# Attention scores from two float32r parts in half of the array's rows, in place of three bfloat16 parts in all of them

## Chip, cores and metric

The kernel runs on one core of a Trainium2 chip. The metric is the device time of one execution in microseconds (us); lower is better. The engines are named as in the profile: PE is TensorE's matmul side and PEld its weight loads, DVE is VectorE, ACT is ScalarE, POOL is GpSimd, SP the engine that issues the DMAs.

## The reference

```python
qn = layer_norm(Q, ln_q_g, ln_q_b)                  # Q: 16 x 512 x 256, all float32
q = (qn @ Wq + bq).reshape(B, 512, 16, 16)          # 16 heads of 16
k = (KV @ Wk + bk).reshape(B, 1601, 16, 16)         # KV: 16 x 1601 x 256
v = (KV @ Wv + bv).reshape(B, 1601, 16, 16)
scores = einsum('bhqd,bhkd->bhqk', q, k) / sqrt(16)
attn = softmax(scores, axis=-1)
ctx = einsum('bhqk,bhkd->bhqd', attn, v)
x = Q + (ctx @ Wo + bo)
h = layer_norm(x, ln_ff_g, ln_ff_b)
out = x + silu(h @ W1 + b1) @ W2 + b2               # W1: 256 x 1024
```

## The kernel before, in words

There are 16 batches. A batch is worked off in 4 quarters of 4 heads, a quarter in 13 key tiles of 128 keys (the last has 65), a tile in two units. So a batch has 52 tiles.

**Scores.** A number of q or k is split into three bfloat16 parts (`k_parts`, `q_parts`). For each head, `k_stack` and `q_stack` hold six blocks of 16 rows, so that one matmul over 96 rows sums the six products of parts that matter. Three more rows hold ones (in `k_stack`) and the negated row maximum in three parts (in `q_stack`), so that the matmul over 99 rows at L1010 gives scores less the maximum, keys on partitions and 512 queries on the free side. ACT takes the exponential of two heads at a time (L717) into `probs`. Then `multiply_v` (L1029) multiplies by v, in float32, for four heads: each head's v has 32 columns, and the four heads go to the four quarters of PSUM's partitions.

**Maxima.** The row maximum has to be known before the scores are made. So PE also makes every score the other way round, queries on partitions (L995: 128 queries by 512 keys, 96 rows), into one of two PSUM buffers (`rows_ps`); DVE reduces each to one column (L830). A quarter has 52 of these steps: 48 of 512 keys and 4 that hold the last 65 keys of four heads. They run up to two quarters ahead, 4 in each tile. At the end of a quarter DVE negates the maxima and splits them (L832 to L844), PE turns them (`turn`, L944), ACT copies them to `shift_parts` and SP places them in `q_stack` (`place_shift`).

**Side work.** All other products of PE go through one PSUM bank, `side`, one step after the other: transposes of context and x (`ctx`, `x`, `h`), the k, q and v projections, the output projection (`wo`), and the two layers of the MLP (`w1`, `w2`). Lists written out by hand (`PREPARE`, `FINISH`, `TURN`) give each step the units in which its products are made. `plan` sets PE's order in a tile: the two score matmuls of a unit first, then the unit's side products, the v product of the tile before at the end of the second unit, and the four maximum matmuls spread by cost among these.

**Stacks.** For k and q, ACT writes the whole number and the first part (L662, L663), POOL makes the second and the third part (L513 to L516), and SP moves the parts to the stacks: 24 small DMAs for the first copies in each quarter's group of heads (`place`), then 6 that copy a block within the stack (`repeat`).

## Time and profile before

| | |
|---|---|
| time, median of 3 runs | 3768.38 us (3765.79 to 3769.14) |
| time of the profiled execution | 3763.43 us |
| its span, first to last instruction | 3761.6 us |
| granted TensorE clock, mean | 0.989 |
| busy share: PE, PEld, DVE, ACT, POOL | 95%, 43%, 66%, 60%, 24% |
| chain that ended last: PE, DVE, ACT | 81%, 11%, 4% |

A quarter takes 53 to 60 us and a batch 224.9 us, the same to a few ns in every batch but the first and the last. PE's busy time counts each matmul until its modelled end, so that matmuls that follow one another closely overlap in it; the distance between two starts says more than the duration.

### The profile page before, as it was taken

Reading aid. Unit: us, or ns where it says so; the run is one execution under the profiler, and the core shown is the slowest. Engines: PE = TensorE matmul, PEld = TensorE weight load, DVE = VectorE, ACT = ScalarE, POOL = GpSimd, SP = SyncE. Lnnn points to the kernel's source line nnn. Section 1 sums busy time; section 2 is a strip of 40 time slices with the busy share of each in tenths; the row PEclk is TensorE's granted clock in tenths of the full one; section 3 lists DMA queues with packets and bytes.
Section 4 is the critical chain, followed back from the end, with each engine's and each line's share of the span. In section 5 each row is a group of like instructions: output and inputs, shape, how many; then the busy total and the mean of one; then the engine's idle time right before and its main releaser. Section 6 shows DMA issues by size and latency. Waiting matters only on the chain.

```text
span 3761.6 us, 52959 instructions
## 1 busy us (share of the span) xinstructions
PE 3559.0 (95%) x19880; PEld 1605.0 (43%) x19880; DVE 2483.2 (66%) x4568; ACT 2242.9 (60%) x2979; POOL 901.5 (24%) x1323
## 2 busy tenths in 40 slices
PE   3899999999999999999999999999999999999996
PEld 2233444444434444444444434444444444444434
DVE  2777767666676766667666676766667676676751
ACT  1366666656666565666656666566656656666562
POOL 2122313212231222313122231212313112231101
PEclk8899999999999999999999999999999999999999
DMA  3222212222122321212222122322212232121200
GB/s 84 45 50 40 46 32 61 41 47 45 32 51 39 65 41 32 47 33 58 41 58 38 30 50 37 64 41 36 49 32 54 42 64 39 27 48 34 41 7 12
DMA packets 121409, 162.99 MB, mean 43 GB/s; under 512 B 36912, under 2 KB 102464, under 8 KB 118080
## 3 DMA queue, kind: packets, MB, share of 16 engines
q1 hardware_dynamic: 121152, 159.60, 21.7%
q8 instruction: 157, 2.57, 0.3%
q14 instruction: 100, 0.82, 0.1%
HBM read 46.43 MB, written 8.39 MB: 15 GB/s over the span
## 4 chain that ended last, share of the span: by engine, by line
PE 81%; DVE 11%; ACT 4%; issue 2%; SPq 1%; POOL 1%; DMA 0%; ACTq 0%; POOLq 0%; DVEq 0%
PE o_ps L1029 20%; PE rows_ps L995 19%; PE scores L1010 14%; DVE chunk_max L830 8%; PE side L972 6%; PE side L969 6%; PE side L958 5%; PE side L950 4%; PE side L962 3%; ACT probs L717 2%; PE side L954 2%; DVE stats L748 1%; DVE resid L775 1%; PE side L941 1%; ACT ctxT L633 1%
## 5 line engine op out<-in xcount | busy, mean ns | idle before, releaser
L830 DVE TENSOR_REDUCE chunk_max<-rows_ps 128x1 f32<-128x512 f32 (+1 forms) x3328 | 2124.4, 666 | 1132.9 <-PE rows_ps L995 1124.4
L717 ACT ACTIVATE probs<-scores 128x1024 f32<-128x1024 f32 (+1 forms) x1664 | 1676.0, 1023 | 1174.5 <-PE scores L1010 1167.1
L995 PE MATMUL rows_ps<-k_stack,q_stack 96*128 96x512 bf16 (+1 forms) x4096 | 1220.1, 339 | 94.1 <-DVE chunk_max L830 50.6
L1010 PE MATMUL scores<-q_stack,k_stack 99*128 99x512 bf16 (+1 forms) x3328 | 1033.6, 379 | 3.3 <-ACT probs L717 2.7
L1029 PE MATMUL o_ps<-probs,v_sb 128*32 128x512 f32 x6656 | 886.5, 605 | 0.4 <-ACT probs L717 0.4
L995 PEld LDWEIGHTS rows_ps<-k_stack,q_stack 96*128 96x128 bf16 x4096 | 334.3, 97 | 1164.2 <-DVE chunk_max L830 930.7
L1010 PEld LDWEIGHTS scores<-q_stack,k_stack 99*128 99x128 bf16 (+1 forms) x3328 | 325.0, 100 | 300.4 <-issue 38.2
L513 POOL TENSOR_TENSOR rest<-whole,k_parts 128x512 f32<-128x512 f32 (+1 forms) x128 | 120.6, 942 | 1002.4 <-ACT k_parts L663 997.2
L565 POOL TENSOR_TENSOR attT<-o_sb,denom 128x512 f32<-128x512 f32 x64 | 81.2, 1268 | 945.3 <-DVE denom L817 945.3
L969 PE MATMUL side<-hT,w_sb 128*128 128x256 f32 x1024 | 272.6, 380 | 11.8 <-ACT tanh_sb L675 9.9
L972 PE MATMUL side<-w_sb,ffT 128*128 128x256 f32 x1024 | 259.2, 381 | 5.6 <-DVE ffT L793 5.0
L1029 PEld LDWEIGHTS o_ps<-probs,v_sb 128*32 128x32 f32 x6656 | 131.0, 108 | 296.8 <-issue 222.2
L958 PE MATMUL side<-wv_sb,ctxT 128*128 128x128 f32 (+1 forms) x1664 | 242.3, 278 | 4.6 <-ACT v_sb L649 2.0
L958 PEld LDWEIGHTS side<-wv_sb,ctxT 128*128 128x128 f32 (+1 forms) x1664 | 226.0, 187 | 46.7 <-ACT v_sb L649 11.4
L950 PE MATMUL side<-ctxT,wk_sb 128*128 128x512 f32 (+1 forms) x512 | 222.7, 519 | 9.2 <-ACT k_parts L663 9.2
L969 PEld LDWEIGHTS side<-hT,w_sb 128*128 128x128 f32 x1024 | 192.9, 190 | 63.2 <-ACT tanh_sb L675 17.0
L972 PEld LDWEIGHTS side<-w_sb,ffT 128*128 128x128 f32 x1024 | 191.5, 189 | 56.5 <-issue 7.7
L673 ACT ACTIVATE ffT<-side,half_b 128x256 f32<-128x256 f32 x256 | 121.5, 475 | 111.5 <-PE side L969 108.8
L528 POOL TENSOR_TENSOR newton<-rstd 128x2 f32<-128x2 f32 (+1 forms) x144 | 28.1, 195 | 591.6 <-DVE half_var L763 584.0
L962 PE MATMUL side<-wo_pad,attT 128*128 128x256 f32 x512 | 139.7, 389 | 5.0 <-POOL attT L565 3.9
L675 ACT ACTIVATE tanh_sb<-side,half_b 128x256 f32<-128x256 f32 x256 | 121.7, 475 | 0.0
L514 POOL TENSOR_TENSOR k_parts<-whole,k_parts 128x512 bf16<-128x512 f32 (+1 forms) x128 | 121.1, 946 | 0.1
(68 smaller groups left out, 1971.3 us busy)
## 6 DMA issues: line engine op xcount, KB each, us to landing
k_stack<-k_parts SPq DMA_DIRECT2D x768, 50.0 KB, 2.2
k_stack<-k_stack SPq DMA_DIRECT2D x192, 200.1 KB, 5.6
ctx_nat<-in_ctx SPq DMA_DIRECT2D x48, 512.0 KB, 4.0
q_stack<-q_parts SPq DMA_DIRECT2D x768, 16.0 KB, 1.8
q_stack<-q_stack SPq DMA_DIRECT2D x192, 64.0 KB, 3.4
x_nat<-in_x SPq DMA_DIRECT2D x16, 512.0 KB, 6.1
resid<-in_x SPq DMA_DIRECT2D x32, 256.0 KB, 2.8
out<-resid SPq DMA_DIRECT2D x32, 256.0 KB, 2.5
```

The costliest lines, as they stand in the source:

```text
L673: nc.scalar.activation(ffT[:, m, :], side[:, cols], ACT.Identity, bias=half_b1[:, m:m + 1], scale=0.5)
L675: last = nc.scalar.activation(tanh_sb[:, cols], side[:, cols], ACT.Tanh, bias=half_b1[:, m:m + 1], scale=0.5)
L717: nc.scalar.activation(probs[0:rows, (q + t) % 2, 2 * LQ * pair:2 * LQ * (pair + 1)], scores[0:rows, 2 * LQ * pair:2 * LQ * (pair + 1)], A ...
L830: nc.vector.tensor_reduce(dst, src, AX.X, ALU.max).then_inc(rows_read, 1)
L950: ins = nc.tensor.matmul(side[:, 0:width(arg)], wk_sb[:, j, P * s:P * (s + 1)], ctxT[:, j, CHUNK * arg:CHUNK * arg + width(arg)], start=(j ...
L958: ins = nc.tensor.matmul(side[0:rows, P * t:P * (t + 1)], ctxT[:, j, P * i:P * i + rows], wv_sb[:, j, P * s:P * (s + 1)], start=(j == 0), ...
L962: ins = nc.tensor.matmul(side[:, D * i:D * (i + 1)], attT[:, j, q0:q0 + P], wo_pad[:, j, :], start=(j == 0), stop=(j == 3))
L969: ins = nc.tensor.matmul(side[:, QH * i:QH * (i + 1)], w1_sb[:, j, P * m:P * (m + 1)], hT[:, j, :], start=(j == 0), stop=(j == KC - 1))
L972: ins = nc.tensor.matmul(side[:, D * i:D * (i + 1)], ffT[:, j, P * i:P * (i + 1)], w2_sb[:, j, :], start=(j == 0), stop=(j == FM - 1))
L995: last = nc.tensor.matmul(rows_ps[:, m % 2, d0:d0 + w], q_stack[s][0:STACK, h, P * t:P * (t + 1)], k_stack[s][0:STACK, h, k0:k0 + w], star ...
L1010: ins = nc.tensor.matmul(scores[0:keys_in(t), LQ * j:LQ * (j + 1)], k_stack[s][:, h, P * t:P * t + keys_in(t)], q_stack[s][:, h, :], start ...
L1029: last = nc.tensor.matmul(o_ps[32 * j:32 * j + 32, :], v_sb[q // 2][0:rows, t, col:col + 32], probs[0:rows, (q + t) % 2, LQ * j:LQ * (j + 1)],
```

## The change

- Each number is split into **two float32r parts** (float32r is a 4-byte type that the matmul reads as it is). Three blocks of 16 rows hold the three products that matter, so a head takes 48 rows for the maxima and 50 for the scores (two rows of shift).
- A head lies in **one half of the array's rows**: even heads in rows 0 to 49, odd heads in rows 64 to 113. A stack is [128, 4 pairs, keys].
- `plan` puts each score matmul **next to a maximum matmul of the other half**, and spreads these pairs: score, maximum, part of the first unit's side products, score, maximum, the rest of them; then score, maximum, v product, score, maximum, the second unit's side products.
- The maximum steps alternate between the halves; the last chunk of keys takes 66 keys in place of 65.
- `read_parts` on POOL is one subtraction in place of three. `repeat` is gone: `place` writes each of the three blocks from `k_parts` and `q_parts` (24 DMAs in a group, of 4-byte numbers). `place_shift` issues four DMAs in place of three.
- Negating the maxima takes three DVE instructions in place of seven; `turn` is one float32 transpose in place of four bfloat16 matmuls, and ACT copies 32 x 128 in place of 12 x 512.
- DVE sets the whole of `k_stack` to one at the start, and SP waits for that before it fills the stacks.

```diff
-PARTS = 3
-K_ROWS = (0, 0, 0, 1, 1, 2)
-Q_ROWS = (0, 1, 2, 0, 1, 0)
+PARTS = 2
+K_ROWS = (0, 0, 1)
+Q_ROWS = (0, 1, 0)
+HALF = 64
+PAIRS = HH // 2
-PLACED = 2 * 4 * PARTS
-REPEATED = 2 * (len(K_ROWS) - PARTS)
+PLACED = 2 * 4 * len(K_ROWS)
...
-TAIL = width(NCH - 1)
-M_STEPS = [step for r in range(M_ROWS) for step in [(r, c) for c in range(NCH - 1)] + [(r, None)] * (r % 4 == 3)]
+TAIL = width(NCH - 1) + 1
+M_STEPS = [step for p in range(2) for step in
+           [(e, p, t, c) for t in range(QT) for c in range(NCH - 1) for e in range(2)] + [(e, p, None, None) for e in range(2)]]
...
+PARTNER = (1, 0, 1, 0)
 def plan(steps):
-    units, slot = [], 0
+    units = []
     for t in range(KT):
-        work = []
-        for u in (2 * t, 2 * t + 1):
-            work += [(u, "scores", j) for j in range(2)]
-            work += [(u, "side", product) for product in products_at(steps, u)]
-            work += [(u, "pv", None)] * (u % 2)
...
+        fill = [[("side", product) for product in products_at(steps, u)] for u in (2 * t, 2 * t + 1)]
+        tile = []
+        for n in range(2):
+            first, second = 2 * n, 2 * n + 1
+            cost = [COST[what[1]] for _, what in fill[n]]
+            cut = 0
+            while cut < len(cost) and sum(cost[:cut]) * 2 < sum(cost):
+                cut += 1
+            middle = [("pv", None)] if n == 1 else fill[n][:cut]
+            unit = [("scores", PARTNER[first]), ("max", PER_TILE * t + first)] + middle
+            unit += [("scores", PARTNER[second]), ("max", PER_TILE * t + second)] + fill[n][0 if n == 1 else cut:]
+            tile.append(unit)
+        units += tile
     return units
...
-        k_stack = [sb(f"k_stack{s}", [ROWS, HH, LK], BF16) for s in range(2)]
+        k_stack = [sb(f"k_stack{s}", [P, PAIRS, LK], F32R) for s in range(2)]
...
             def place(dst, src, rows, g):
-                for part in range(PARTS):
-                    slot = rows.index(part)
+                for slot, part in enumerate(rows):
                     for h in range(4 * (g % 2), 4 * (g % 2) + 4):
-                        sp.dma_start(dst[16 * slot:16 * slot + 16, h, :], src[16 * h:16 * h + 16, part, :])\
-                            .then_inc(placed[g], 16)
+                        first = HALF * (h % 2) + 16 * slot
+                        sp.dma_start(dst[first:first + 16, h // 2, :].bitcast(F32),
+                                     src[16 * h:16 * h + 16, part, :].bitcast(F32)).then_inc(placed[g], 16)
...
-                repeat(b, 2 * s)
                 place(q_stack[s], q_parts, Q_ROWS, 2 * s + 1)
-                repeat(b, 2 * s + 1)
...
+                sp.wait_ge(ones_set, 4)
                 fill_stacks(0, 0)
...
-                wait(pool, split, b * 10 + n)
-                seq.inc(nc.gpsimd.tensor_tensor(rest[:, 0:w], src, first, ALU.subtract))
-                seq.inc(nc.gpsimd.tensor_tensor(second, src, first, ALU.subtract))
-                pool.wait_ge(pool_seq, seq.value)
-                nc.gpsimd.tensor_tensor(parts[:, 2, off:off + w], rest[:, 0:w], second, ALU.subtract).then_inc(split, 1)
+                nc.gpsimd.tensor_tensor(parts[:, 1, off:off + w], whole[:, n % 2, 0:w],
+                                        parts[:, 0, off:off + w].bitcast(F32), ALU.subtract).then_inc(split, 1)
...
             def make_rows(b, q, m):
-                r, c = M_STEPS[m]
-                s = q // 2
+                e, p, t, c = M_STEPS[m]
+                s, pair, rows = q // 2, 2 * (q % 2) + p, slice(HALF * e, HALF * e + STACK)
...
-                    last = nc.tensor.matmul(rows_ps[:, m % 2, d0:d0 + w], q_stack[s][0:STACK, h, P * t:P * (t + 1)],
-                                            k_stack[s][0:STACK, h, k0:k0 + w], start=True, stop=True)
+                    last = nc.tensor.matmul(rows_ps[:, m % 2, d0:d0 + w], q_stack[s][rows, pair, P * tile:P * (tile + 1)],
+                                            k_stack[s][rows, pair, k0:k0 + w], start=True, stop=True)
...
             def make_scores(b, q, u, n, first):
...
-                j = 2 * (u % 2) + n
-                h = 4 * (q % 2) + j
+                j, pair, rows = 2 * (u % 2) + n, 2 * (q % 2) + u % 2, slice(HALF * n, HALF * n + ROWS)
                 ins = nc.tensor.matmul(scores[0:keys_in(t), LQ * j:LQ * (j + 1)],
-                                       k_stack[s][:, h, P * t:P * t + keys_in(t)], q_stack[s][:, h, :],
+                                       k_stack[s][rows, pair, P * t:P * t + keys_in(t)], q_stack[s][rows, pair, :],
                                        start=True, stop=True)
```

## Rows read from the trace of the kernel before

**Rows 1.** The page: busy time by engine, clock in 40 slices, start of the chain.
```profile
PE 3559.0 (95%) x19880; PEld 1605.0 (43%) x19880; DVE 2483.2 (66%) x4568; ACT 2242.9 (60%) x2979; POOL 901.5 (24%) x1323
...
PEclk8899999999999999999999999999999999999999
...
PE 81%; DVE 11%; ACT 4%; issue 2%; SPq 1%; POOL 1%; DMA 0%; ACTq 0%; POOLq 0%; DVEq 0%
```

**Rows 2.** Groups by form: count, busy us and mean ns, idle before and releaser.
```profile
L830 DVE TENSOR_REDUCE chunk_max<-rows_ps 128x1 f32<-128x512 f32 x3072 | 2028.2, 687 | 1036.4 <-PE rows_ps L995 1027.9
L717 ACT ACTIVATE probs<-scores 128x1024 f32<-128x1024 f32 x1536 | 1550.1, 1024 | 1095.2 <-PE scores L1010 1087.8
...
L995 PEld LDWEIGHTS rows_ps<-k_stack,q_stack 96*128 96x128 bf16 x4096 | 334.3, 97 | 1164.2 <-DVE chunk_max L830 930.7 <-issue 152.2
...
L969 PEld LDWEIGHTS side<-hT,w_sb 128*128 128x128 f32 x1024 | 192.9, 190 | 63.2 <-ACT tanh_sb L675 17.0 <-ACT hT L641 1.4 <-DVE resid L775 1.2
...
L941 PEld LDWEIGHTS side<-ident,ctx_nat 128*128 128x128 f32 x384 | 46.7, 145 | 54.5 <-ACT ctxT L633 27.9 <-issue 21.2
```

**Rows 3.** Timeline of PE through one tile with two k products.
```profile
2225.99 0.60 PE L1010 MATMUL scores<-q_stack,k_stack 99*128 99x512 bf16 x2
2226.42 0.38 PE L995 MATMUL rows_ps<-k_stack,q_stack 96*128 96x512 bf16 x1
2226.64 1.02 PE L950 MATMUL side<-ctxT,wk_sb 128*128 128x512 f32 x2
2227.50 0.38 PE L995 MATMUL rows_ps<-k_stack,q_stack 96*128 96x512 bf16 x1
2227.72 0.60 PE L1010 MATMUL scores<-q_stack,k_stack 99*128 99x512 bf16 x2
...
2229.01 0.38 PE L995 MATMUL rows_ps<-k_stack,q_stack 96*128 96x512 bf16 x1
2229.32 1.06 PE L1029 MATMUL o_ps<-probs,v_sb 128*32 128x512 f32 x8
2230.32 0.39 PE L995 MATMUL rows_ps<-k_stack,q_stack 96*128 96x512 bf16 x1
```

**Rows 4.** Timeline of PE around one `turn` (weights of 12 columns).
```profile
2135.25 0.38 PE L995 MATMUL rows_ps<-k_stack,q_stack 96*128 96x512 bf16 x1
2135.56 0.39 PE L944 MATMUL side<-ident_bf,neg_parts 128*12 128x128 bf16 x4
2135.88 0.39 PE L1010 MATMUL scores<-q_stack,k_stack 99*128 99x512 bf16 x1
```

**Rows 5.** Busy us of each engine in single tiles of one batch.
```profile
core 0: us, PE busy (x) PEld busy (x) DVE busy (x) ACT busy (x) POOL busy (x), PEclk, DMA share, GB/s
2168.69:2172.07 3.38, 2.92 (x20) 0.78 (x19) 2.60 (x6) 1.89 (x2) 2.23 (x11) 1.00 0.60 124
2172.07:2175.18 3.11, 3.02 (x17) 0.75 (x16) 2.26 (x5) 1.99 (x3) 2.88 (x4) 1.00 0.10 26
...
2242.57:2245.84 3.27, 3.27 (x22) 1.00 (x21) 2.26 (x5) 2.39 (x3) 0.00 (x0) 1.00 0.00 0
2155.68:2159.80 4.12, 4.12 (x27) 2.00 (x25) 2.46 (x4) 1.94 (x2) 0.00 (x0) 1.00 0.38 72
2225.99:2230.55 4.56, 4.56 (x22) 1.61 (x21) 2.73 (x4) 3.28 (x5) 3.37 (x3) 1.00 0.02 4
2151.05:2155.68 4.63, 4.63 (x34) 2.97 (x33) 2.76 (x5) 2.64 (x3) 3.72 (x3) 1.00 0.10 25
2197.32:2201.54 4.22, 3.87 (x28) 1.76 (x27) 2.92 (x5) 3.74 (x6) 2.54 (x2) 1.00 0.44 140
```

**Rows 6.** The start: DMAs as SP issues them, and POOL's first split.
```profile
67.92 7.84 SPq L389 DMA_DIRECT2D q_stack<-q_parts  x12
75.81 7.54 SPq L389 DMA_DIRECT2D k_stack<-k_parts  x12
83.39 2.52 SPq L401 DMA_DIRECT2D k_stack<-k_stack  x3
85.94 3.74 SPq L401 DMA_DIRECT2D q_stack<-q_stack  x3
...
64.39 1.16 POOL L513 TENSOR_TENSOR rest<-whole,q_parts 128x512 f32<-128x512 f32 x1 [4.97 <-ACT q_parts L663]
65.50 1.16 POOL L514 TENSOR_TENSOR q_parts<-whole,q_parts 128x512 bf16<-128x512 f32 x1
66.74 1.16 POOL L516 TENSOR_TENSOR q_parts<-rest,q_parts 128x512 bf16<-128x512 f32 x1
```

**Rows 7.** SP's queue just before the quarter that starts at 2141.45.
```profile
2136.95 1.81 SPq L424 DMA_DIRECT2D q_stack<-shift_parts  x3
```

**Rows 8.** Busy us of each engine in the first quarter of that batch, and four quarters' sum.
```profile
2141.45:2197.32 55.87, 53.62 (x321) 25.55 (x320) 39.74 (x79) 30.53 (x38) 13.60 (x32) 1.00 0.41 76
...
sum 224.91, PE 219.48 PEld 99.90 DVE 153.86 ACT 140.12 POOL 56.01; mean PE 54.87 PEld 24.97 DVE 38.46 ACT 35.03 POOL 14.00
```

**Rows 9.** Chain that ended last: the first score matmuls of the first quarter.
```profile
145.66 0.85 PE scores L1010 x2
```

More of the change, by code:

```diff
@@ L28 @@
 F32 = mybir.dt.float32
-BF16 = mybir.dt.bfloat16
+F32R = mybir.dt.float32r
 I32 = mybir.dt.int32
@@ L128, in products @@
         return [(t, kc) for t in tiles_in(c) for kc in (range(KC) if kind == "v" else [arg[1]])]
-    first, second = {"turn": (QT, 1), "x": (QT, 1), "k": (1, KC), "q": (1, KC), "wo": (2, 4), "h": (KC, 2), "w1": (2, KC), "w2": (2, FM)}[kind]
+    first, second = {"turn": (1, 1), "x": (QT, 1), "k": (1, KC), "q": (1, KC), "wo": (2, 4), "h": (KC, 2), "w1": (2, KC), "w2": (2, FM)}[kind]
     return [(i, j) for i in range(first) for j in range(second)]
@@ L165, in maxima @@
     return b + (q + ahead) // 4, (q + ahead) % 4, m
-COST = {"scores": 512, "pv": 2048, "v": 512, "ctx": 256, "x": 256, "h": 256, "turn": 128, "k": 2048, "q": 2048,
+COST = {"pv": 2048, "v": 512, "ctx": 256, "x": 256, "h": 256, "turn": 128, "k": 2048, "q": 2048,
         "wo": 1024, "w1": 1024, "w2": 1024}
+PARTNER = (1, 0, 1, 0)
 def plan(steps):
-    units, slot = [], 0
+    units = []
     for t in range(KT):
-        work = []
-        for u in (2 * t, 2 * t + 1):
-            work += [(u, "scores", j) for j in range(2)]
-            work += [(u, "side", product) for product in products_at(steps, u)]
-            work += [(u, "pv", None)] * (u % 2)
-        costs = [COST[what[1] if kind == "side" else kind] for _, kind, what in work]
-        done, placed, tile = 0, 0, {2 * t: [], 2 * t + 1: []}
-        for (u, kind, what), cost in zip(work, costs):
-            tile[u].append((kind, what))
-            done += cost
-            while placed < PER_TILE and done * PER_TILE >= (placed + MAX_PHASE) * sum(costs):
-                tile[u].append(("max", slot))
-                placed, slot = placed + 1, slot + 1
-        units += [tile[2 * t], tile[2 * t + 1]]
+        fill = [[("side", product) for product in products_at(steps, u)] for u in (2 * t, 2 * t + 1)]
[11 more added lines that the diff above has]
+        units += tile
     return units
@@ L310, in xattn_kernel @@
         placed = [sem(f"placed{g}") for g in range(4)]
-        stack_landed = [sem(f"stack_landed{g}") for g in range(4)]
         scores_ready = sem("scores_ready")
@@ L634, in side_step @@
                 elif kind == "turn":
-                    last = nc.scalar.copy(shift_parts[:, :], side[0:4 * PARTS, :])
+                    last = nc.scalar.copy(shift_parts[:, :], side[0:PARTS * M_ROWS, 0:P])
                 elif kind == "x":
@@ L943, in side_product @@
                 elif kind == "turn":
-                    ins = nc.tensor.matmul(side[0:4 * PARTS, P * i:P * (i + 1)],
-                                           neg_parts[:, i, :, :].rearrange("p a h -> p (a h)"), ident_bf[:, :],
-                                           start=True, stop=True)
+                    ins = nc.tensor.transpose(side[0:PARTS * M_ROWS, 0:P],
+                                              neg_parts[:, :, :].bitcast(F32).rearrange("p a r -> p (a r)"), ident[:, :])
                 elif kind == "x":
@@ L1034, in prologue @@
             def prologue():
-                pe.wait_ge(ident_made, 3)
+                pe.wait_ge(ident_made, 2)
                 n, m = 0, 0
```

76 lines of the change are left out of this document (30 added, 46 removed).

## The prediction

> **What bounds the kernel now.** I read the page first, then the groups of instructions by form, then timelines of single tiles. The page says that PE is busy for 95% of the span and carries 81% of the chain that ended last, with DVE at 66% and ACT at 60% busy [rows 1]. The two groups that the change halves in array rows are large: the groups by form show DVE's reductions and ACT's exponentials waiting for exactly these two PE lines [rows 2]. The timeline of a tile shows PE's true cost, start to start. A score matmul takes 0.215 us and a maximum matmul 0.22 (2226.42 to 2226.64), a k product of two records 0.86 (2226.64 to 2227.50) [rows 3]. Four of each kind make 1.74 us of a tile.
>
> The same rows show a second cost. From the maximum matmul to the v product it is 0.31, not 0.22 (2229.01 to 2229.32), and the v block takes 1.00 until the next matmul starts (2229.32 to 2230.32) [rows 3]. The v product is the one that uses 32-column weights. The turn, with weights of 12 columns, shows it too: 0.31 into it (2135.25 to 2135.56), and 0.32 for four small matmuls and the way out [rows 4]. So PE stops for about 0.095 us each time the shape of the array's tiles changes, on the way in and on the way out.
>
> Not every tile is bound by PE. One with two k products is: 4.56 us of which PE is busy 4.56, and the sum 1.74 + 1.72 + 0.10 + 1.00 gives the same 4.56 [rows 3, 5]. A tile without side work takes 3.11 to 3.38 us with PE idle for part of it, although its PE sum is only about 2.8; there four DVE reductions of 0.687 us (2.75 us) and two exponentials (2.05 us) set the pace [rows 2, 5].
>
> **The change, part by part.** I count per batch of 52 tiles (224.9 us) [rows 8] and call a run of side products between two pairs a group.
>
> *Pairs.* If float32r streams as bfloat16 does and the two halves run together, a pair costs one matmul, 0.222 us. Four pairs are 0.89 in place of 1.74: 0.85 less per tile. That two tiles of the array run together is shown by the v product: eight float32 records of 512 columns in 1.00 us, where a k product takes 0.86 for two [rows 3]. No row shows float32r. The bounds are the bfloat16 row (0.215) and the float32 row (0.86 per product) [rows 3]. I take 0.215, since a part is read once, in one instruction.
>
> *Changes of shape.* A head in half of the rows is a new shape beside the full array and the 32-column one. The trace has no change between 128 and 64 rows; its bounds are nothing (score and maximum matmuls of 99 and 96 rows follow each other at 0.22) and the 0.095 us above [rows 3]. I take 0.095. The v block has its two changes already. Each group adds two.
>
> The Trainium skill says so in TensorEngine Tiling (Array Packing), section Tiling Modes: changing the mode, not just the tile, drains the engine. The trace agrees for columns (0.31 against 0.22); for rows no run so far shows it. By the rule the sum stands as below, without it the first rival holds.
>
> *Weights after a change.* In a stream the load of the next weights is hidden behind the running matmul. After a stop it is not. Loads last 97 ns (bfloat16, 128 columns), 145 (float32, one record per product) and 190 (float32, two records) [rows 2]; so against bfloat16's exposed 0.01 us, the float32 ones show about 0.055 and 0.105. For float32r weights I take 0.055, the one-record row; 0.105 is the other end. A group then costs 0.095 + 0.105 in and 0.095 + 0.055 out, 0.35 us; a group of transposes 0.30. The way out of the v block gets 0.05 dearer.
>
> *Sum of PE's work.* A tile with g groups changes by -0.85 + 0.05 + 0.35 g: -0.80 with none, -0.45, -0.10, and +0.25 with three. Written out from the lists and the new `plan`, a batch has 6 tiles with no group, 11 with one (7 of them transposes), 18 with two, 17 with three (3 all transposes, 1 mixed): 98 groups, 21 of transposes. PE's sum falls by 52 x 0.80 - 77 x 0.35 - 21 x 0.30 = 8.3 us per batch.
>
> *What of it can be cashed.* The large gains are in the light tiles, and DVE stops them at about 3.1 us. Six tiles without a group go from 3.11 to 3.38 to about 3.1: -1.0 in all. Seven with one group of transposes, such as the one of 3.27 [rows 5], give -1.3; four with one other group, such as the one of 4.12 that PE fills [rows 5], -1.75. The 18 with two give -1.7, two of them being held by ACT or DVE. The 17 with three, such as the one of 4.63 that PE fills, would lose 3.8; in tiles where PE waits for ACT's copies (4.22 us with PE busy 3.87) [rows 5] the stops lie in that wait, so I take +2.75. The 16 steps with the last keys were cheaper than 0.22 before and are about 0.28 now: +1.5. Together -1.5 us.
>
> *Shift.* Before, SP issued three DMAs until 2138.76, and the quarter starts at 2141.45, 2.7 us later [rows 7, 8]. A fourth DMA adds 0.6 and the last tiles are shorter; where the landing takes 2 us this becomes a wait of some tenths: +0.5 per batch. What is late then is the first pair of the quarter, and all of PE behind it. The shorter negation, `turn` and copy on DVE, PE and ACT give back about as much as they cost elsewhere: they lie beside side work, nothing.
>
> *POOL and SP.* POOL's two subtractions less, and 48 DMAs in place of 60 per pair of quarters, lie beside PE's work in steady state: nothing. At the start they do not. The first maxima wait for 12 + 12 + 6 DMAs, from 67.92 to 89.7, and POOL's three steps before (64.39 to 67.9) [rows 6]. Now 12 DMAs follow one step: 14 + 2.3 us less, and some 4 more for the k chunks before. DVE's longer setting of the stack lies beside loads. I take 18 us.
>
> *Total.* 15.5 batches at -1.0, and -18: 34 us less than the profiled execution's 3763.4 (span 3761.6 and 1.8 around it), which is 3729. The median of the runs is 5 us above the profiled one, so 3735.
>
> **Rivals.**
>
> *Rows change shape for nothing.* Then groups cost nothing and a tile is worth up to 0.85. For it: 96 and 99 rows follow each other without a stop [rows 3]; against it: both column cases stop. The light tiles stay at 3.1, the 35 with two or three groups gain 0.8 unless ACT or DVE holds them, the 11 others about half: 20 us per batch, 3768 - 320 = 3450 with the start.
>
> *Dearer weights (the other side).* At each of 150 entries into pairs per batch the exposed load is 0.105 in place of 0.055, or the loads of the two halves follow each other. For it: the two-record float32 load is at 190 ns; against it: the four loads of the v product go together. 0.05 x 150 = 7.5 us, of which 6 in tiles that PE fills: +94, so 3830; both at once would be 3920. It decides when the exposed load is above 0.075 us, where the 34 us are gone.
>
> *The pair costs two matmuls.* Either float32r streams at half the rate, or the maximum matmul waits and the halves don't meet. Then the tile has before's matmul time again and the stops on top: 52 x 0.05 + 33 = 36 us per batch, 32 of it paid, 4280. At float32's 0.86 for each it would be above 5600.
>
> A page bears on the rate: the Trainium skill, FP8 and Floating Point Precision, section TensorE Precision Notes, has full float32 in four passes and a reduced mode that reads the 4-byte number and cuts it. Two records at 0.43 each agree with four passes of 0.215; one pass for the reduced mode would be the forecast's sum.
>
> **Numbers.** About 0.2% (7 us) is what this kernel's measurement can tell from no change. The forecast's mechanism (stops paid, cheap weights) 0.40, its own range 3690 to 3800, of it 0.26 faster, 0.04 within, 0.10 slower. Dearer or serial weights 0.23, all slower but 0.01 within. No stop for rows 0.20, faster. A pair at two matmuls or more 0.17, slower. That makes faster 0.46, within 0.05, slower 0.49. The range from 3430 to 3920 takes in the first three cases.
>
> **What would show it.** After the change the distance of a score matmul to its maximum matmul is some 10 ns, a pair takes 0.22, from a pair to a side product it is 0.31 or more, the weights of L995 and L1010 load in about 145 ns, and light tiles take 3.1 us with PE waiting for DVE. Tiles with three groups are longer than before, those with one shorter. The first quarter starts at about 128 us in place of 145.7 [rows 9]. The forecast is wrong if the distance into a side product stays at 0.22 (first rival), if the weights last 190 ns (second), or if pairs are 0.43 apart (third).

## The result and the profile after

The changed kernel takes 4489.76 us (median of 4 runs, 4472.48 to 4515.56), the kernel before 3767.09 beside it: a ratio of 1.1925, 95% interval 1.1863 to 1.1986. The forecast was 3735 us with a range of 3430 to 3920. The profiled execution is the one of 4515.56 us, its span 4513.5.

The page of the changed kernel: busy time by engine and the granted clock in 40 slices.

```profile
PE 4159.6 (92%) x19688; PEld 1863.5 (41%) x19688; DVE 2495.3 (55%) x4312; ACT 2268.3 (50%) x2979; POOL 615.2 (14%) x1002
PEclk8899999798887987998788989798997979997778
```

Against [rows 1], two lines matter. DVE and ACT have about the work they had before, spread over a longer span. PE's share of busy time hardly moved. The clock row did: before, it shows 9 from the third slice on, now it falls to 8 and 7 all through the kernel. The mean granted clock is 0.873 against 0.989. The windows of single tiles below show a granted clock of 1.00 or 0.50, that is 2.4 or 1.2 GHz. If every stretch runs at one of these two, the share of the span at 1.2 GHz is twice what the mean lacks: 2 x 0.127 x 4513.5 = 1146 us, against 2 x 0.011 x 3761.6 = 83 us before. I call this the low time of a run; each run below has one.

Groups of instructions by form, of the changed kernel (count, busy us and mean ns, idle before and its releaser):

```profile
L817 DVE TENSOR_REDUCE chunk_max<-rows_ps 128x1 f32<-128x512 f32 x3072 | 2044.5, 687 | 1497.5 <-PE rows_ps L974 1487.7
L703 ACT ACTIVATE probs<-scores 128x1024 f32<-128x1024 f32 x1536 | 1562.4, 1024 | 1926.8 <-PE scores L988 1925.5
L974 PEld LDWEIGHTS rows_ps<-k_stack,q_stack 48*128 48x128 f32 x4096 | 718.1, 205 | 275.3 <-DVE chunk_max L817 259.4 <-issue 5.8 <-DMA q_stack<-q_parts 0.8
```

DVE and ACT wait for the two changed PE lines, as before and for longer. A load of the float32r weights lasts 205 ns here, where the bfloat16 one took 97 [rows 2].

Timeline of PE in the changed kernel, through the tile with two k products that answers to [rows 3] (start, duration, instruction, and in brackets the idle time before it with what ended it):

```profile
2654.31 0.49 PE L988 MATMUL scores<-q_stack,k_stack 50*128 50x512 f32 x1
...
2655.74 1.12 PE L931 MATMUL side<-ctxT,wk_sb 128*128 128x512 f32 x2 [0.93 <-ACT k_parts L649]
...
2658.45 0.50 PE L988 MATMUL scores<-q_stack,k_stack 50*128 50x512 f32 x1
2658.46 0.49 PE L974 MATMUL rows_ps<-k_stack,q_stack 48*128 48x512 f32 x1
2658.88 1.12 PE L931 MATMUL side<-ctxT,wk_sb 128*128 128x512 f32 x2
2659.94 0.50 PE L988 MATMUL scores<-q_stack,k_stack 50*128 50x512 f32 x1
```

The pair does what it should: score and maximum matmul start within 10 ns of each other (2658.45 and 2658.46). But from a pair to a side product it is 0.42 us (2658.46 to 2658.88). Before, two matmuls one behind the other took 0.43 to the same place, so this pair saves nothing. And ahead of the first k product PE stands still for 0.93 us, for ACT. ACT in that stretch:

```profile
2654.42 0.69 ACT L648 ACTIVATE whole<-side,bk_c 128x512 f32<-128x512 f32 x1
2655.01 0.68 ACT L649 ACTIVATE k_parts<-side,bk_c 128x512 fp32r<-128x512 f32 x1
```

The side product before this one must be copied out by two activations, 1.3 us together, before the next may write `side`. Only one pair, 0.43 us, lies between the two products.

Windows of single tiles of the changed kernel, in the form of [rows 5]: two light tiles (one at either level of the clock; the second holds one small matmul, the turn), the k tile above, one with a v product, one with transposes of the context.

```profile
2581.86:2586.65 4.79, 4.79 (x18) 1.89 (x16) 2.58 (x4) 1.94 (x2) 1.27 (x1) 0.50 0.00 0
2674.93:2678.26 3.33, 3.33 (x20) 1.28 (x17) 2.57 (x4) 2.07 (x3) 0.00 (x0) 1.00 0.00 0
2654.31:2659.94 5.63, 4.70 (x21) 1.42 (x21) 2.67 (x4) 3.32 (x5) 1.27 (x1) 1.00 0.01 3
2556.56:2561.96 5.40, 5.15 (x34) 2.91 (x34) 2.77 (x4) 2.64 (x4) 3.00 (x3) 1.00 0.24 53
2624.53:2631.61 7.08, 7.08 (x27) 2.65 (x26) 4.25 (x7) 3.60 (x6) 1.27 (x1) 0.50 0.25 76
```

At full clock the k tile has gone from 4.56 us to 5.63, the v tile from 4.63 to 5.40, and the light tile has won nothing (3.33 against 3.11 to 3.38). At half clock (0.50 in the clock column) a light tile takes 4.79, and one with transposes 7.08 where [rows 5] has 4.22.

The four quarters of that batch:

```profile
2546.18:2617.10 70.92, 68.38 (x320) 32.66 (x317) 39.49 (x75) 31.55 (x38) 14.88 (x33) 0.78 0.31 65
2617.10:2682.91 65.81, 60.59 (x287) 23.66 (x283) 39.82 (x71) 38.96 (x52) 14.14 (x23) 0.87 0.06 18
2682.91:2753.58 70.67, 65.35 (x345) 32.23 (x341) 39.24 (x63) 36.13 (x50) 2.23 (x2) 0.93 0.28 53
2753.58:2815.83 62.25, 58.47 (x293) 25.11 (x289) 37.37 (x61) 35.29 (x46) 6.66 (x6) 1.00 0.03 8
```

Together 269.7 us, against 224.9 for a batch before [rows 8]. The last quarter has full clock throughout and takes 62.25 us, where the same quarter took 56.13 before; four times 62.25 is 249. So there are two questions: what costs more than 20 us per batch at full clock, and what takes the clock away.

### The profile page after: what moved, and what is told of

It is laid out like the page before. It is cut to its first block, busy times and chain, and to the rows that moved or that the text cites. A ratio compares the mean times of both kernels' runs of the same rounds, so it can differ in the third digit from the quotient of the medians.

```text
span 4513.5 us, 51519 instructions
## 1 busy us (share of the span) xinstructions
PE 4159.6 (92%) x19688; PEld 1863.5 (41%) x19688; DVE 2495.3 (55%) x4312; ACT 2268.3 (50%) x2979; POOL 615.2 (14%) x1002
## 4 chain that ended last, share of the span: by engine, by line
PE 83%; ACT 7%; DVE 5%; issue 3%; SPq 1%; DMA 1%; POOL 0%; ACTq 0%; POOLq 0%; DVEq 0%
PE scores L988 22%; PE o_ps L1007 21%; PE rows_ps L974 9%; PE side L950 7%; PE side L939 6%; PE side L953 6%; PE side L931 5%; PE side L943 3%; DVE chunk_max L817 3%; PE side L935 2%; PE side L923 2%; ACT k_parts L649 1%; ACT tanh_sb L661 1%; ACT probs L703 1%; ACT ffT L659 1%
## 5 line engine op out<-in xcount | busy, mean ns | idle before, releaser
L974 PE MATMUL rows_ps<-k_stack,q_stack 48*128 48x512 f32 (+1 forms) x4096 | 1685.8, 473 | 94.3 <-DVE chunk_max L817 91.6
L988 PE MATMUL scores<-q_stack,k_stack 50*128 50x512 f32 (+1 forms) x3328 | 1586.1, 519 | 7.1 <-ACT probs L703 7.1
L988 PEld LDWEIGHTS scores<-q_stack,k_stack 50*128 50x128 f32 (+1 forms) x3328 | 622.6, 201 | 1390.8 <-issue 1255.7
L1007 PE MATMUL o_ps<-probs,v_sb 128*32 128x512 f32 x6656 | 1038.7, 701 | 1.1 <-ACT probs L703 1.1
L974 PEld LDWEIGHTS rows_ps<-k_stack,q_stack 48*128 48x128 f32 x4096 | 718.1, 205 | 275.3 <-DVE chunk_max L817 259.4
L950 PE MATMUL side<-hT,w_sb 128*128 128x256 f32 x1024 | 344.8, 456 | 44.6 <-ACT tanh_sb L661 27.5
L931 PE MATMUL side<-ctxT,wk_sb 128*128 128x512 f32 (+1 forms) x512 | 260.8, 596 | 88.3 <-ACT k_parts L649 88.3
L503 POOL TENSOR_TENSOR k_parts<-whole,k_parts 128x512 fp32r<-128x512 f32 (+1 forms) x128 | 132.1, 1033 | 1494.2 <-ACT k_parts L649 1494.2
L779 DVE SCALAR_TENSOR_TENSOR ffT<-tanh_sb,ffT 128x512 f32<-128x512 f32 x128 | 95.6, 747 | 125.5 <-ACT tanh_sb L661 125.5
L931 PEld LDWEIGHTS side<-ctxT,wk_sb 128*128 128x128 f32 x512 | 81.8, 199 | 161.9 <-ACT k_parts L649 116.7
L923 PE MATMUL side<-ident,ctx_nat 128*128 128x128 f32 (+1 forms) x416 | 103.2, 356 | 41.9 <-DMA ctx_nat<-in_ctx 27.1
```

The lines of the kernel that those rows point to most:

```text
L923: ins = nc.tensor.transpose(side[:, P * t:P * t + rows], ctx_nat[0:rows, c % 2, t, P * j:P * (j + 1)], ident[0:rows, 0:rows])
L931: ins = nc.tensor.matmul(side[:, 0:width(arg)], wk_sb[:, j, P * s:P * (s + 1)], ctxT[:, j, CHUNK * arg:CHUNK * arg + width(arg)], start=(j ...
L950: ins = nc.tensor.matmul(side[:, QH * i:QH * (i + 1)], w1_sb[:, j, P * m:P * (m + 1)], hT[:, j, :], start=(j == 0), stop=(j == KC - 1))
L974: last = nc.tensor.matmul(rows_ps[:, m % 2, d0:d0 + w], q_stack[s][rows, pair, P * tile:P * (tile + 1)], k_stack[s][rows, pair, k0:k0 + w] ...
L988: ins = nc.tensor.matmul(scores[0:keys_in(t), LQ * j:LQ * (j + 1)], k_stack[s][rows, pair, P * t:P * t + keys_in(t)], q_stack[s][rows, pai ...
L1007: last = nc.tensor.matmul(o_ps[32 * j:32 * j + 32, :], v_sb[q // 2][0:rows, t, col:col + 32], probs[0:rows, (q + t) % 2, LQ * j:LQ * (j + 1)],
```

## Experiments

The change has three parts that can be had alone: the written order of a tile (`plan` and `PARTNER`), the number format, and the halves of the array. The first runs take them apart.

**The order alone.** The kernel before, with three bfloat16 parts in all rows, and the changed kernel's order.

```
-def plan(steps):
+PARTNER = (0, 1, 0, 1)
...
+        fill = [[("side", product) for product in products_at(steps, u)] for u in (2 * t, 2 * t + 1)]
...
+            middle = [("pv", None)] if n == 1 else fill[n][:cut]
+            unit = [("scores", PARTNER[first]), ("max", PER_TILE * t + first)] + middle
+            unit += [("scores", PARTNER[second]), ("max", PER_TILE * t + second)] + fill[n][0 if n == 1 else cut:]
```

> The kernel before (three bfloat16 parts, whole array) with nothing changed but the order of plan: score, maximum, side products, score, maximum, side products; score, maximum, v product, score, maximum, side products. No new shapes of tile, no float32r. Theory A (the new order takes away the cover of ACT's copies out of the side bank, because a side step now often ends just ahead of the next step's first product): slower than before by about 8 us per batch, 3890 us, with PE waiting for ACT at the side lines for some 130 us. Theory B (all the loss is changes of shape, weights and clock): within 0.5% of before, 3767.

Measured: 4005.5 us, ratio 1.0631 (1.0615 to 1.0647), clock 0.987. The order alone costs 238 us, with neither float32r nor halves nor a lower clock. The direction was expected, the size was not (3890). PE in its k tile:

```profile
2358.59 0.38 PE L996 MATMUL rows_ps<-k_stack,q_stack 96*128 96x512 bf16 x1
2359.89 1.13 PE L951 MATMUL side<-ctxT,wk_sb 128*128 128x512 f32 x2 [0.92 <-ACT k_parts L664]
```

The same idle time ahead of the k product. The view of waits of PE has it in sum (us in total, times, longest):

```profile
PE side L951 <- ACT k_parts L664: 92.5, 93, 7.0
PE rows_ps L996 <- DVE chunk_max L831: 52.5, 132, 1.2
```

The changed kernel has 88.3 us at the same place. And the kernel before:

```profile
PE side L950 <- ACT k_parts L663: 9.2, 3, 6.4
PE rows_ps L995 <- DVE chunk_max L830: 50.6, 157, 0.9
```

All of PE's waits for ACT ahead of side products, summed from this view, are 215 us in order_only and 43 before. That is 172 of the 238 us. The waits for DVE ahead of the maxima have not grown (52.5 against 50.6). The other 66 us were not traced.

**Halves without float32r.** The changed kernel with two bfloat16 parts per number. They carry 8 bits each, some 16 bits of the number, where the three parts of before and the float32r parts carry more.

```
-F32R = mybir.dt.float32r
+F32R = mybir.dt.bfloat16
...
-                ins = nc.tensor.transpose(side[0:PARTS * M_ROWS, 0:P],
...
+                    ins = nc.tensor.matmul(side[0:PARTS * M_ROWS, 0:P], neg_parts[:, :, :].rearrange("p a r -> p (a r)"),
+                                           ident_bf[:, :], start=True, stop=True)
```

> The changed kernel with every float32r tile made bfloat16: two parts of 8 bits, so the scores carry about 16 bits, the products, rows, halves, pairs and order as in the changed kernel. It tells the type from the halves. Theory A (float32r's exposed weight loads cost 0.1 us at each of 150 entries into pairs per batch): the weights take 97 ns in place of 205, 150 x 0.1 = 15 us per batch less in PE's work, some 10 of it paid, so about 4330 if the clock stays as low, near 4000 if it does not fall. Theory B (float32r is slow in its stream or lowers the clock by itself): pairs get shorter and the granted clock goes back to 0.98, about 3900. Theory C (halves and stops lower the clock): clock stays near 0.88.

Measured: 3935.65 us, ratio 1.0453 (1.0436 to 1.0469), clock 0.967. That is 70 us below order_only and 554 below the changed kernel. Its timeline of PE:

```profile
1999.78 0.39 PE L991 MATMUL scores<-q_stack,k_stack 50*128 50x512 bf16 x1
1999.78 0.39 PE L977 MATMUL rows_ps<-k_stack,q_stack 48*128 48x512 bf16 x1
2000.10 0.70 PE L946 MATMUL side<-wo_pad,attT 128*128 128x256 f32 x2
2000.73 0.39 PE L991 MATMUL scores<-q_stack,k_stack 50*128 50x512 bf16 x1
```

From the pair to a side product, with 128 columns on both sides and only the rows changed, it is 0.32 us (1999.78 to 2000.10): 0.215 and a stop of 0.10. The stop for a change of rows, which the trace of before could not show, is there. The way back takes 0.63 (2000.10 to 2000.73) for two records of 0.215, so 0.20 more: the second stop and the side product's own exposed float32 weights. Together a group costs 0.30 us here. The clock is nearer to full than the changed kernel's, so halves alone do not account for its fall. Of the three expectations the second comes nearest in time and clock, but its ground, float32r as slow or as what lowers the clock by itself, falls with the next run.

**float32r without halves.** The matmuls read rows 0 to 111, both heads at once, so the scores of two heads are added up and the result is no longer this attention's.

```
-                s, pair, rows = q // 2, 2 * (q % 2) + p, slice(HALF * e, HALF * e + STACK)
+                s, pair, rows = q // 2, 2 * (q % 2) + p, slice(0, HALF + STACK)
...
-                j, pair, rows = 2 * (u % 2) + n, 2 * (q % 2) + u % 2, slice(HALF * n, HALF * n + ROWS)
+                j, pair, rows = 2 * (u % 2) + n, 2 * (q % 2) + u % 2, slice(0, HALF + STACK)
```

> The changed kernel with its matmuls over rows 0 to 111, so that each score and maximum matmul covers both halves and adds up the two heads of a pair: the output is not the reference's. Order, float32r and all other engines as in the changed kernel; pairs no longer run side by side, but no change of shape besides the v product's either. If float32r streams one column in a clock as bfloat16 does and its weights hide in a stream: matmul distance 0.22 us, PE's work as in the kernel before, time near that of the order-only run, 3800 to 3900, clock 0.98. If float32r costs more per column: 0.43 us distance and above 4600. If float32r lowers the clock, it is low here too.

Measured: 4170.61 us, ratio 1.1073 (1.1054 to 1.1091), clock 0.990. Its timeline of PE:

```profile
1999.68 0.50 PE L989 MATMUL scores<-q_stack,k_stack 112*128 112x512 f32 x1
2000.02 0.40 PE L975 MATMUL rows_ps<-k_stack,q_stack 112*128 112x512 f32 x1
2000.25 0.39 PE L989 MATMUL scores<-q_stack,k_stack 112*128 112x512 f32 x1
2000.48 0.40 PE L975 MATMUL rows_ps<-k_stack,q_stack 112*128 112x512 f32 x1
2000.71 1.03 PE L951 MATMUL side<-hT,w_sb 128*128 128x256 f32 x4
```

float32r streams 512 columns in 0.23 us, almost as bfloat16 (0.215 to 0.22). The rival of half the rate is out. Here the step into the side product is 0.23 too: all rows before and after, no change of shape, no stop. Behind the v block it is 0.34 (1999.68 to 2000.02): the next float32r weights are exposed there. The time was expected at 3800 to 3900 and came out higher. An estimate from these rows: 52 exposed loads of 0.107 and 416 matmuls that are about 0.0125 longer make 10.8 us per batch, 167 us in 15.5 batches, against the 165 by which this run is above order_only.

These three give a first account. (Runs with two parts also have POOL's and SP's lighter work, which lies in these differences.) From 3768: the order +238, float32r in the whole array +165 (4171 less 4005), the halves -70. That makes 4101. Measured are 4490; 389 us are in none of the parts alone. The low time says where to look: 83 us before, some 105 for order_only, 83 for f32r_whole, 260 for bf16_halves, 1146 for all together.

**All side work between the pairs.** To give ACT's copies cover, I put all fill of a unit between its two pairs.

```
-            middle = [("pv", None)] if n == 1 else fill[n][:cut]
+            middle = fill[n] + [("pv", None)] * n
...
-            unit += [("scores", PARTNER[second]), ("max", PER_TILE * t + second)] + fill[n][0 if n == 1 else cut:]
+            unit += [("scores", PARTNER[second]), ("max", PER_TILE * t + second)]
```

> The changed kernel with another order: score, maximum, all side products of the first unit, score, maximum; score, maximum, side products of the second unit and right behind them the v product, score, maximum. A tile has 5 to 6 changes of shape in place of 8, and the v product covers ACT's copies again. Theory A (order and number of stops carry the loss at full clock): 20 us per batch less, and 4170 or less; if the clock then stays up, about 3750 to 3850. Theory B (the clock falls for another reason): clock near 0.88, 4200.

Measured: 4957.72 us, ratio 1.3169 (1.3128 to 1.321), clock 0.842. I had expected 4170 or less. It got worse by 468 us, and the timeline of PE and ACT shows why:

```profile
2928.27 0.40 PE L988 MATMUL scores<-q_stack,k_stack 50*128 50x512 f32 x1
2928.46 1.02 ACT L703 ACTIVATE probs<-scores 128x1024 f32<-128x1024 f32 x1 [3.33 <-PE scores L988]
2929.38 0.68 ACT L648 ACTIVATE whole<-side,bk_c 128x512 f32<-128x512 f32 x1
2929.95 0.69 ACT L649 ACTIVATE k_parts<-side,bk_c 128x512 fp32r<-128x512 f32 x1
2930.70 1.54 PE L931 MATMUL side<-ctxT,wk_sb 128*128 128x512 f32 x2 [2.03 <-ACT k_parts L649]
```

The exponential takes both scores of a unit in one instruction, and the second now comes after the fill. In ACT's order the copies of the fill stand behind that exponential (2929.38 and 2929.95, behind 2928.46), and PE waits 2.03 us for them. The wait at this line is 188.5 us in all. An order must put both scores of a unit ahead of its fill.

**Both pairs first.** So the next order has both scores first in every unit, then the fill.

```
+            unit = [("scores", 0), ("scores", 1), ("max", PER_TILE * t + first), ("max", PER_TILE * t + second)]
+            unit += fill[n] + [("pv", None)] * n
```

I ran it in three formats: float32r halves (first_f32r), two bfloat16 halves (first_bf16), and before's three parts in all rows (first_whole).

> The changed kernel with pairs of another kind: at the start of each unit the two score matmuls (one in each half), then two maximum matmuls (one in each half), then the unit's side products, then in the second unit the v product. The exponential can start as early as in the kernel before, a side step is followed by two pairs or the v product, and a tile has at most 5 changes of shape in place of 8. Theory A (the order delays the exponential and with it ACT's copies out of the side bank, and the stops and exposed weights do the rest; the clock follows from PE's waiting): the waits for ACT at the side lines fall from 130 us to under 50, the clock returns to 0.97 or more, and the time is 3600 to 3750. Theory B (float32r in halves lowers the clock whatever the order): clock under 0.92 and over 4000.

> The same order with the bfloat16 parts of the run bf16_halves (two parts of 8 bits). Against first_f32r it has the weight loads of 0.094 us in place of 0.2. Theory A (exposed weights cost about 0.1 us at 3 entries into pairs or fewer per tile): 10 us per batch less in PE's sum than first_f32r, some of it hidden behind DVE: 3450 to 3600. Theory B (only the order counts): within 2% of first_f32r.

> The kernel before (three bfloat16 parts, whole array) in the same order: two scores, two maxima, side products, v product last. It is the control for the two runs beside it. Theory A: two maxima one behind the other wait a little more for DVE, 3780 to 3850, and not the 4005 of the other order; the difference to order_only is what the late exponential costs. Theory B (any grouping of maxima starves DVE and costs as much): about 4000.

Measured: first_f32r 4052.28 us, ratio 1.0777 (1.0716 to 1.0838), clock 0.934; first_bf16 3772.65, ratio 1.0009 (0.9993 to 1.0024), clock 0.973; first_whole 3897.34, ratio 1.0342 (1.0326 to 1.0357), clock 0.986. Against the changed kernel's order that is -438, -163 and -108. All three are slower than I had expected of this order (3600 to 3750, 3450 to 3600, 3780 to 3850). The wait for ACT at the k products is 8.3 us again in first_f32r. This order has a loss of another kind, which the waits of PE show, here of first_whole:

```profile
PE rows_ps L995 <- DVE chunk_max L830: 164.6, 471, 1.5
```

In first_whole PE's waits for ACT ahead of side products are down to 34 us, below the 43 of before, but its waits for DVE have gone from 50.6 to 164.6: 114 of the 130 us by which it is slower than before. First_f32r has 213.5 us of them. So the 238 us of order_only and the 130 of first_whole are not one loss and a part of it; they are two different ones, waits for ACT and waits for DVE.

Two maximum matmuls in a row fill both buffers of `rows_ps` while DVE's reduction takes 0.687 us. The plan of before placed each maximum by the costs of the work between; every order in pairs gives that up, and pays where maxima meet.

**Fewer columns for DVE.** The changed kernel, with each reduction reading half of its chunk; the maximum of the other half is left out.

```
-                    dst, src = chunk_max[:, r + t, c:c + 1], rows_ps[:, m % 2, :]
+                    dst, src = chunk_max[:, r + t, c:c + 1], rows_ps[:, m % 2, 0:CHUNK // 2]
```

> The changed kernel with DVE reducing only the first 256 of the 512 columns of each maximum step (half of the maximum's work on DVE left out), PE's instructions unchanged. Light tiles no longer wait for DVE. Theory A (the clock falls where PE waits for DVE and ACT in light tiles): the slow stretches in the first quarter of a batch go, granted clock above 0.95, about 4150. Theory B (pairs and stops alone lower the clock): clock stays near 0.88 and the time within 2% of the changed kernel's 4490.

Measured: 4212.98 us, ratio 1.1183 (1.1161 to 1.1204), clock 0.931. PE's work is the same to the instruction, yet 277 us are gone and the low time is 581 instead of 1146. DVE has a hand in the pace of the light tiles and, with it, in how densely PE works in them. How much of the 277 us comes through the clock this run can't tell by itself; at the price that old_order gives below it would be some 220.

**More work for PE.** The changed kernel, with each score matmul of the 22 light tiles of a batch issued twice: 88 more matmuls per batch.

```
+        light = sum(COST[what[1]] for part in fill for _, what in part) <= 2048
+        tile = [[("again" if light and kind == "scores" else kind, what) for kind, what in unit] for unit in tile]
```

> The changed kernel in which every score matmul is issued twice in the 22 tiles per batch with little side work (the second writes the same numbers again: 88 matmuls of 0.215 us per batch more, 300 us of PE time in all). Theory A (the clock falls because the array streams too little in these tiles): the slow stretches shrink to under 300 us in all, clock above 0.95, and the kernel is faster by 100 to 250 us in spite of the added work: 4250 to 4390. Theory B (the clock falls from pairs, that is from too much work at once, or independent of the load): slow stretches stay above 1000 us and the time rises to 4600 or more.

Measured: 4391.41 us, ratio 1.1657 (1.1627 to 1.1687), clock 0.949. Work was only added, and the kernel is 98 us faster than the changed one; the low time fell from 1146 to 447 us, not quite to the 300 that I had expected. So the clock is a cause and not a symptom, and it does not fall from too much work.

**The arithmetic in the old order.** The changed kernel with before's `plan`.

```
-        fill = [[("side", product) for product in products_at(steps, u)] for u in (2 * t, 2 * t + 1)]
...
+            while placed < PER_TILE and done * PER_TILE >= (placed + MAX_PHASE) * sum(costs):
+                tile[u].append(("max", slot))
+                placed, slot = placed + 1, slot + 1
```

> The changed kernel with plan as it was before: both scores first, maxima spread one by one among the side products, v product at the end of the second unit. Float32r and halves as changed, so the two scores still run side by side, but a maximum matmul stands alone between side products and brings its own changes of shape: up to 10 in a tile. Theory A (the order's missing cover is a large part): the waits for ACT's copies go, PE's sum is 1 us per tile higher from stops and lone maxima, so 4100 to 4300, below the changed kernel only because of the cover. Theory B (stops are what costs): more stops, so above 4490, with the clock as low or lower.

Measured: a median of 4386.2 us; its four runs lie 3.4% apart, so no ratio is given. They are useful all the same, since the same instructions ran at four mean clocks: 4439.64 us at 0.899, 4407.02 at 0.908, 4365.37 at 0.919, 4292.89 at 0.940. The low time goes from 896 us to 515, the time by 147: 0.39 us of time per us of low clock. The changed kernel's own four runs give 43 us for 118 (0.36), first_f32r's 55 for 136 (0.41), cover's 39 for 122 (0.32). The run also says what the order is worth in the changed formats. With before's own `plan` the kernel still takes 4293 to 4440 us, more than 520 above before. A lone maximum matmul between side products has its own changes of shape, up to 10 in a tile. So giving the old order back does not rescue the change.

**Maxima on both sides.** The last order keeps both scores of a unit first and puts one maximum ahead of them, one behind them, and one more behind the v product.

```
+        unit = [("max", PER_TILE * t + 1)] * n + [("scores", 0), ("scores", 1), ("max", PER_TILE * t + 2 * n)]
+        unit += fill[n] + [("pv", None), ("max", PER_TILE * t + 3)] * n
```

> As first_f32r, but the maxima stand on both sides of the two scores: first unit score, score, maximum, side products; second unit maximum, score, score, maximum, side products, v product, maximum. 5 changes of shape, exponential early, and the maxima of a tile are further apart. Theory A (first_f32r's 207 us of PE and 550 us of weight loads waiting for DVE come from maxima in twos): waits for DVE fall by half, 3850 to 3950. Theory B (DVE paces these tiles anyway): within 1% of first_f32r's 4052.

> The same order as straddle_f32r with two bfloat16 parts. Theory A: 3600 to 3700, faster than the kernel before. Theory B: as first_bf16, 3770.

Measured: straddle_f32r 3962.56 us, ratio 1.0513 (1.0465 to 1.0562), clock 0.946; straddle_bf16 3674.11 us, ratio 0.975 (0.9735 to 0.9764), clock 0.969. The latter is the only one of the twelve that is faster than before, by 94 us, with scores from some 16 bits of each number. Its k tile in the timeline of PE:

```profile
2158.64 0.39 PE L976 MATMUL rows_ps<-k_stack,q_stack 48*128 48x512 bf16 x1
2158.64 0.60 PE L990 MATMUL scores<-q_stack,k_stack 50*128 50x512 bf16 x2
2158.87 0.38 PE L976 MATMUL rows_ps<-k_stack,q_stack 48*128 48x512 bf16 x1
2159.17 1.12 PE L933 MATMUL side<-ctxT,wk_sb 128*128 128x512 f32 x2
...
2162.83 0.39 PE L976 MATMUL rows_ps<-k_stack,q_stack 48*128 48x512 bf16 x1
```

The tile takes 4.19 us (2158.64 to 2162.83) in place of 4.56, PE never stands idle in it, and the number of stops has fallen since pairs meet in groups of two. With bfloat16 this order is 98 us faster than first_bf16, and PE's waits for DVE at the maxima are down from 329.5 us to 249.5. With float32r it is 90 us faster than first_f32r, but these waits, which I had expected to fall by half, are 220.9 us against 213.5; where its 90 us come from is not shown. Against straddle_bf16, float32r adds 288 us. Straddle_f32r is the best order tried for float32r halves, and it is still 195 us slower than the kernel before.

## Why the prediction was wrong

**The pair and the rate were right.** Two halves run side by side (starts within 10 ns), and float32r streams 512 columns in 0.23 us. The third rival is out.

**The stop was right.** A change of rows stops PE as one of columns does: 0.32 in place of 0.215 from a pair to a side product in bf16_halves. The first rival (no stop, 3450 us) is out. The Trainium skill, TensorEngine Tiling (Array Packing), section Tiling Modes, says that a change of tiling mode drains the engine, and this is the run that shows it for rows.

**The exposed weights were mis-sized.** The prediction took 0.055 us for a float32r load after a stop. The loads last 182 to 205 ns, and from a pair to a product of another shape it is 0.42 to 0.43 (2658.46 to 2658.88) where the bfloat16 halves need 0.32: 0.107 per entry. That is the second rival's value, above the 0.075 at which its side wins. It shows once per run of matmuls of one shape: in f32r_whole the first is followed after 0.34 us, the next ones after 0.23. It also shows behind a wait of PE (2574.14 to 2574.57 below), which the prediction didn't count. A group costs 0.41 in place of 0.35. By the prediction's own sum the 0.05 at 150 entries are the rival's +94 us. The format's price by runs is 165 us with whole rows, 280 in the both-pairs-first order and 288 in the last order, the latter two with some of the clock in them.

**The order was taken as free; this is the first step that failed.** "What of it can be cashed" weighed each tile by its sum of PE's work plus stops, as if the matmuls could be set in any order at no cost, and even laid stops into "tiles where PE waits for ACT's copies". The view was there: [rows 5] shows the tile of 4.22 us with PE busy for 3.87. The question I didn't ask was what covers ACT's 1.3 us of copying when side products close one tile and open the next after a single pair. The order alone costs 238 us, of which 172 are further waits of PE for ACT ahead of side products. Moving the side work behind both pairs takes these waits away and puts 114 us of waits for DVE at the maxima in their place (first_whole), so neither order in pairs is free. The prediction's forecast for the batch was -1.0 us; order_only's batch is 239.4 us in place of 224.9, +14.5.

**The clock was not in the sum; this is the second.** The prediction costs every tile at the clock of before (0.989). In the changed kernel it falls in light tiles, and side work behind them then runs at the lower level too. PE's timeline around a fall:

```profile
2571.91 0.49 PE L988 MATMUL scores<-q_stack,k_stack 50*128 50x512 f32 x1
2571.91 0.72 PE L974 MATMUL rows_ps<-k_stack,q_stack 48*128 48x512 f32 x2
2572.25 0.62 PE L988 MATMUL scores<-q_stack,k_stack 50*128 50x512 f32 x2
2574.14 0.49 PE L974 MATMUL rows_ps<-k_stack,q_stack 48*128 48x512 f32 x1 [1.28 <-DVE chunk_max L817]
2574.57 1.07 PE L1007 MATMUL o_ps<-probs,v_sb 128*32 128x512 f32 x8
...
2577.10 0.79 PE L988 MATMUL scores<-q_stack,k_stack 50*128 50x512 f32 x1
2577.10 1.21 PE L974 MATMUL rows_ps<-k_stack,q_stack 48*128 48x512 f32 x2
2577.69 1.05 PE L988 MATMUL scores<-q_stack,k_stack 50*128 50x512 f32 x2
```

The windows on both sides of it:

```profile
2571.91:2575.56 3.65, 2.37 (x15) 0.82 (x14) 3.47 (x10) 1.09 (x2) 0.00 (x0) 1.00 0.23 51
2577.10:2581.26 4.16, 4.16 (x15) 1.31 (x14) 1.98 (x3) 1.35 (x3) 3.44 (x10) 0.50 0.11 24
```

The busy records hide how little is streamed. A pair ahead of another shape occupies 0.42 us, of which 0.215 is streaming; the rest is stop and load. In the 3.65 us from 2571.91 to 2575.56 there are three pairs (0.65 us) and a v block (0.99), with a wait of 1.28 us for DVE between them: 1.64 us, less than half. Over the whole kernel the page says 92% busy. At 2577.10 the next pair follows after 0.59 us and not after 0.34, and the window's clock is 0.50: 1.2 GHz.

The additive account leaves 389 us. The median run of the changed kernel has a clock of about 0.88, which is 1078 us of low time; the parts alone, added in the same way, make 83 + 23 - 23 + 154 = 237. The other 841 us at 0.36 us each, as its own runs give, are an estimated 305 of the 389. The last 85 or so were not measured apart. One candidate is of the right size: the halves create 98 further entries per batch (the groups) at which float32r's weights are exposed, 98 x 0.107 x 15.5 = 163 us of PE's work, part of it hidden in waits. That the clock costs time is shown by repeat_light, in which more work is faster. That the deep fall takes both parts is shown by f32r_whole (0.990), bf16_halves (0.967) and both (0.873). Which measure of PE's activity decides the fall is not settled.

The Trainium skill, TensorE: Matmul & The Clock Gate, section HAM oscillation, has the clock fall over gaps in PE's work, over long ones and, in one kernel, over many short ones. The runs here do not line up by gaps. The longest wait in the tiles ahead of the fall shown was 1.28 us. And PE's waits, summed from the view, are 344 us in the changed kernel and 451 in bf16_halves, whose clock is higher (0.967 against 0.873). Short_reads and repeat_light can't decide it: they make PE's work denser and also shorten its waits for DVE, from 91.6 us to 34.7 and 34.0. So gaps are not all that counts here, and what else does is open.

**The light tiles** stayed near the forecast at full clock (3.33 us in the one shown, forecast 3.1), but where the clock is down they take 4.79. **The start** came in part: the chain of the changed kernel has its first score matmul of the first quarter here, at 133.6 us against 145.7 [rows 9] and the forecast's 128, so 12 us of the 18.

```profile
133.64 0.43 PE scores L988
```

**A rival of the other side** was priced with dearer weights at 3830, and with serial loads too at 3920. Its first mechanism holds. Its second is not seen: the weight loads of both halves start together, at 2571.91 in the stretch above. Neither price reaches 4490; the order and the clock, which no rival had, make up some 540 of the 722 us (238 measured, 305 estimated).

## What to carry to other kernels

Halving the rows of a matmul saves its stream only. Before counting on it, count the changes of shape, each with its stop and its exposed load, and set that (here 0.30 us per group with bfloat16 pairs, 0.41 with float32r, both around float32 side products) against the 0.215 that a pair saves; then put as many pairs together as the buffers allow.

When a change rewrites the order of an in-order engine's work, price that first and alone: for each product ask how long the engine that copies it out needs, and what PE has to do until then. The same holds for the engine that empties the buffers of the maxima. A run with only the new order would have shown a third of the loss.

When PE's work gets lighter in tiles that another engine paces, look at the row of the granted clock. A saving on PE can be paid back at half clock, and a busy share of 92% doesn't exclude it.

## What the runs showed of the hardware that I had not expected

float32r matmuls stream like bfloat16 (0.23 us for 512 columns), but their weights load like float32's two-record ones: 182 to 205 ns against 97 for bfloat16 and 190 for two float32 records [rows 2]. Hidden in a stream, they show with 0.107 us at each change of shape, and as much behind a wait (0.42 from 2574.14 to 2574.57, where the bfloat16 halves have 0.32).

The clock fell to 1.2 GHz for a quarter of the span in a kernel whose PE is busy for 92% of it, and 88 added matmuls per batch gave more than half of that back. At the lower level each us of such time costs 0.32 to 0.41 us, less than the half that would be lost if PE alone set the pace throughout. That DVE and ACT pace part of these tiles would explain it; no run shows it by itself.
